# Projected q/k blocks: one ScalarE read of the PSUM bank, the rest formed by VectorE from the bank

## The reference, cut to what matters

```python
q = _split_heads(x @ Wq + bq)
k = _split_heads(x @ Wk + bk)
v = _split_heads(x @ Wv + bv)
scores = jnp.einsum('bhqd,bhkd->bhqk', q, k) / math.sqrt(HEAD_DIM)
```

## Time and profile before

| | value |
|---|---|
| median of 3 runs | 999.82 us |
| the profiled execution, its own time | 999.01 us |
| its span, first to last instruction | 997.1 us |
| TensorE matmul busy | 855.4 us (86%) |
| VectorE busy | 542.0 us (54%) |
| ScalarE busy | 421.5 us (42%) |
| GpSimd busy | 304.6 us (31%) |
| mean granted TensorE clock | 0.922 of full speed |

### The profile page before, as it was taken

The page is one execution under the profiler, slowest core; times in us unless marked ns, Lnnn a source line. Parts: engine busy times, 40 slices in busy tenths (PEclk is TensorE's granted clock), DMA queues, the critical chain, the costliest instruction groups (busy, mean ns, idle before and its releaser), DMA issues. The chain is left out here.

```text
span 997.1 us, 14099 instructions
## 1 busy us (share of the span) xinstructions
PE 855.4 (86%) x4842; PEld 541.8 (54%) x4842; DVE 542.0 (54%) x2095; ACT 421.5 (42%) x741; POOL 304.6 (31%) x365
## 2 busy tenths in 40 slices
PE   6979999898898899899889798349999999999940
PEld 2655556545455455355445243236877877877830
DVE  1268535779798799799878777410211211210136
ACT  1315434587585586686455556113021021022005
POOL 6113223434334333222253423460203212302332
PEclk9998999999799799899799689669999999999975
DMA  9652211202202202201321301631145135233242
GB/s 345 207 188 65 59 29 48 81 1 66 65 2 65 65 1 65 66 23 44 86 84 43 106 7 61 223 116 43 16 127 143 22 122 143 27 120 71 27 110 84
DMA packets 57510, 81.48 MB, mean 82 GB/s; under 512 B 6624, under 2 KB 51041, under 8 KB 55008
## 3 DMA queue, kind: packets, MB, share of 16 engines
q1 hardware_dynamic: 49520, 70.48, 22.0%
q0 software_dynamic: 7296, 9.47, 5.7%
q10 hardware_dynamic: 624, 0.63, 0.2%
HBM read 35.37 MB, written 19.68 MB: 55 GB/s over the span
## 5 line engine op out<-in xcount | busy, mean ns | idle before, releaser
L1102 DVE CUSTOM_DVE_ANT_0 junk<-ps,maskb 128x256 bf16<-128x256 f32 (+4 forms) x512 | 205.8, 434 | 66.3 <-PE ps L821 64.9
L647 ACT ACTIVATE probs<-ps 128x512 f32<-128x512 f32 (+1 forms) x304 | 157.4, 552 | 95.6 <-PE ps L844 91.3
L1559 PE MATMUL ps<-dxT,qs 128*128 128x320 f32 x512 | 141.1, 436 | 1.3 <-DVE dxT L1633 1.3
L1571 PE MATMUL ps<-ks,hTe 128*128 128x256 f32 x640 | 139.3, 379 | 0.0
L1593 ACT ACTIVATE hTe<-ps,qs 128x640 f32<-128x640 f32 x64 | 50.8, 793 | 204.6 <-PE ps L1559 204.6
L1515 POOL DMA_INDIRECT mixed_rows<-ysb,ids x40 | 61.7, 1543 | 228.1 <-DVE ysb L1653 225.2
L1571 PEld LDWEIGHTS ps<-ks,hTe 128*128 128x128 f32 x640 | 121.1, 190 | 16.3
L1559 PEld LDWEIGHTS ps<-dxT,qs 128*128 128x128 f32 x512 | 97.9, 192 | 42.5 <-DVE dxT L1633 1.9
L844 PE MATMUL ps<-qs,ks 99*128 99x256 bf16 (+4 forms) x512 | 107.7, 296 | 15.3 <-DVE nmax L1102 9.0
L821 PE MATMUL ps<-ks,qs 96*128 96x256 bf16 (+4 forms) x512 | 108.8, 299 | 12.6 <-DVE nmax L1102 7.3
L860 PE MATMUL ps<-probs,vaug 128*32 128x256 f32 (+4 forms) x1024 | 92.6, 437 | 6.2 <-POOL probs L557 5.6
(11 more groups left out here) (188 smaller groups left out, 1193.0 us busy)
## 6 DMA issues: line engine op xcount, KB each, us to landing
qs<-parts SPq DMA_DIRECT2D x96, 128.0 KB, 2.4
ks<-parts SPq DMA_DIRECT2D x96, 128.0 KB, 2.4
qs<-w SPq DMA_DIRECT2D x8, 1024.0 KB, 9.5
ks<-w SPq DMA_DIRECT2D x8, 1024.0 KB, 4.9
dispatched_rows<-att SPq DMA_DIRECT2D x8, 650.0 KB, 10.4
ks<-dispatched_rows SPq DMA_DIRECT2D x4, 650.0 KB, 7.2
x_sb<-xT SPq DMA_DIRECT2D x8, 256.0 KB, 3.9
mixed_rows<-h SPq DMA_DIRECT2D x4, 512.0 KB, 3.3
```

The costliest lines, as they stand in the source:

```text
L647: act.activation(probs_of(u)[:, heads[0]:heads[-1] + 1, :], turned_bank((u, half, i))[:, 0:len(heads) * w].rearrange("p (j n) -> p j n", n=w),
L1102: ins = dve.tensor_tensor_reduce(out=junk[:, b - (b > V_BANK), a * (hi - lo):(a + 1) * (hi - lo)], in0=score_bank((u, half, i))[:, a * (hi ...
L1559: ins = mm(bank(2 * (n % 2) + c)[:, 0:HC], w1s[:, e % 2, k, m * P:(m + 1) * P], dxT[:, e % 2, k, c * HC:(c + 1) * HC], start=(k == 0), sto ...
L1571: ins = mm(bank(4 + n % 2)[:, 0:D], hTe[:, e % 2, m, t * P:(t + 1) * P], w2s[:, e % 2, m, :], start=(m == 0), stop=(m == MH - 1))
```

## The change

ScalarE reads the bank once, into part 0, with the bias and without a scale; it no longer writes `proj` and no longer waits for `part2_done`. VectorE forms the rest straight from the bank, (bank + bias) - part 0, as one `scalar_tensor_tensor` into `proj`; that instruction now gives the bank free, and it takes over the wait for `part2_done`. The factor 1/4 goes into the q weights, which VectorE multiplies once per layer. Part 0 gets a semaphore of its own, on which SyncE and VectorE wait. The planner is told that a q/k bank is read one half later.

```diff
-READ_LATER = {"tok": {"h": 1}, "ffn": {"u": HIDDEN}, "gate": {"l": 1}, "route": {"c": 1}, "bias": {"o": 0}}
+READ_LATER = {"qkv": {"q": 1}, "tok": {"h": 1}, "ffn": {"u": HIDDEN}, "gate": {"l": 1}, "route": {"c": 1}, "bias": {"o": 0}}
...
                         if part == 0:
-                            sp.wait_ge(*d_out(("qkv", s, f"qk{i}")))
+                            sp.wait_ge(part0_done, 2 * NB * s + i + 1)
...
-                            pool.wait_ge(rest_done, n + 1)
+                            pool.wait_ge(*d_out(("qkv", i, f"qk{c - 2}")))
                             pool.tensor_copy(parts[:, c - 2, 1, :], proj[:, c % 2, :]).then_inc(part1_done, 1)
...
-                                if 2 * NB * i + j >= 2:
-                                    act.wait_ge(part2_done, 2 * NB * i + j - 1)
                                 if i:
                                     q = NB * (i - 1) + j // 2
                                     act.wait_ge(stack_in[q % NR], STACKED * (q // NR + 1))
-                                kw = dict(bias=ab[l][:, j:j + 1], scale=1.0 if j % 2 else DH ** -0.5)
-                                act.activation(proj[:, j % 2, :], dense_bank(key), ACT.Identity, **kw)
                                 act.activation(parts[:, j, 0, :], dense_bank(key), ACT.Identity,
-                                               **kw).then_inc(d_out(key)[0], 1)
+                                               bias=ab[l][:, j:j + 1]).then_inc(part0_done, 1)
...
-                                    if i == 0:
-                                        pe.wait_ge(for_a0, 16 * 2)
-                                    if i == B:
-                                        pe.wait_ge(for_rest, 16 * 9)
+                                    if i % B == 0:
+                                        pe.wait_ge(weights_scaled, l + 1)
...
-                                dve.wait_ge(*d_out(("qkv", i, f"qk{j}")))
-                                dve.tensor_tensor(proj[:, j % 2, :], proj[:, j % 2, :], parts[:, j, 0, :],
-                                                  ALU.subtract).then_inc(rest_done, 1)
+                                key = ("qkv", i, f"qk{j}")
+                                dve.wait_ge(part0_done, 2 * NB * i + j + 1)
+                                if 2 * NB * i + j >= 2:
+                                    dve.wait_ge(part2_done, 2 * NB * i + j - 1)
+                                dve.scalar_tensor_tensor(proj[:, j % 2, :], dense_bank(key), ab[i // B][:, j:j + 1],
+                                                         parts[:, j, 0, :], ALU.add, ALU.subtract
+                                                         ).then_inc(d_out(key)[0], 1)
...
+                                    dve.tensor_scalar(aw[1][:, :, 0:D], aw[1][:, :, 0:D], DH ** -0.5, None,
+                                                      ALU.mult).then_inc(weights_scaled, 1)
...
+                            dve.tensor_scalar(aw[0][:, :, 0:D], aw[0][:, :, 0:D], DH ** -0.5, None,
+                                              ALU.mult).then_inc(weights_scaled, 1)
```

More of the change, by code:

```diff
@@ L299, in build @@
         stack_in = [sem(f"stack_in{i}") for i in range(NR)]
-        rest_done, part1_done, part2_done, bias_added = (
-            sem(n) for n in ("rest_done", "part1_done", "part2_done", "bias_added"))
+        part0_done, part1_done, part2_done, bias_added, weights_scaled = (
+            sem(n) for n in ("part0_done", "part1_done", "part2_done", "bias_added", "weights_scaled"))
         ln_chain, var_done, rstd_done, ln_done = (sem(n) for n in ("ln_chain", "var_done", "rstd_done", "ln_done"))
```

## The result

The changed kernel takes **1029.79 us** (median of 4 runs, 1028.73 to 1032.16) against 999.4 (996.51 to 1000.0) for the kernel before: ratio 1.0312, 95% interval 1.0288 to 1.0335. The forecast was 1010.7, its range 994.5 to 1022. The direction was right; the loss is 30.4 us where 10.9 was forecast, and the time lies above the range.

The account below looks back on a forecast made before the run. TensorE and VectorE together were taken to bound projections 3 to 6. Terms -2.8 - 1.3 + 0.3 + 10.5 + 3.0 + 1.2 = +10.9 us on 999.01, plus 0.8 to the median, gave 1010.7 us, range 994.5 to 1022.

Parts of the forecast that it names:

- The mechanism: From projection 2 on, banks stay held until VectorE's rest, two halves on; planner told one, so TensorE and VectorE wait.
- same-half wait: Projections 3, 5, 6: five banks handed on in the half VectorE reads them; 2.1 us each, 10.5 us (0 to 15.5).
- next-half wait: Projections 4 to 6: six waits, bank handed on the half after VectorE's read; 0.5 us each, 3.0 us (0 to 14.4).
- VectorE's rest costs about the same: VectorE's 32 rests, now straight from the bank: 740 ns against 782, -1.3 us (-3.3 to +5.6).
- Weights: One VectorE instruction per layer scaling the q weights, hidden in layer 0: +0.3 us (0 to 0.69).
- ScalarE busy "some 22 us less": Profile sign: without 32 ScalarE reads of 684 ns, ScalarE's busy time falls by some 22 us.
- Projection 7: Turned scores wait for VectorE's rest while waits for GpSimd and ScalarE's second read go: +1.2 us (0 to 4.1).
- rival C: Much slower: new waits drop TensorE's clock to 1.2 GHz in a quarter of four stretches; 1023 us, chance 0.13.
- ScalarE's relief: ScalarE loses a read and a wait, returning VectorE's waits for it in projections 3 to 6: -2.8 us.
- small terms: Terms besides bank waits: ScalarE's lost read and wait -2.8, VectorE's rest -1.3, weight scaling +0.3 us.
- A: Faster: ScalarE was the hidden holder; half of TensorE's idle time in projections 3 to 7 returns, 995 us, chance 0.22.
- B: No change: bank waits come at half size and returned ScalarE time pays for them; 1000 us, chance 0.10.

Follow-up runs that it names:

- experiment 11: Kernel before, with only VectorE's rest put one half earlier in projections 2 to 7; ScalarE still reads twice: 996.61 us, ratio 0.9976.
- experiment 1: Changed kernel, planner told that q/k banks of projections 2 to 7 are read two halves later: 999.09 us, ratio 1.0002.
- experiment 2: Kernel before with only the new entry in the planner's table; ScalarE still frees the banks: 998.44 us, ratio 0.9995.
- experiment 3: Kernel before with the new table and the bank freed by VectorE's rest, old arithmetic and both ScalarE reads kept: 1032.09 us, ratio 1.0333.
- experiment 5: Changed kernel, planner never takes a bank in the half in which VectorE reads it, or sooner: 1012.08 us, ratio 1.0142.
- experiment 8: Changed kernel, planner told two halves for projections 2 to 7 except projection 6, told one: 1007.88 us, ratio 1.011.
- experiment 4: Kernel before without ScalarE's read into proj and its wait for part 2; rest formed from a constant tile: 995.03 us, ratio 0.9955.
- experiment 7: Changed kernel, rest formed one half after the product in projections 2 to 7, planner told two halves: 993.07 us, ratio 0.9938.
- experiment 6: Changed kernel, rest formed one half after the product instead of two in projections 2 to 7, table unchanged: 990.52 us, ratio 0.9933.
- experiment 9: Changed kernel, planner told two halves for projections 2 to 7 except projection 3, told one: 1004.33 us, ratio 1.0054.

## Why the prediction was right in direction and short in size

The mechanism came out as forecast; what failed is the size of its two terms, the price of a same-half wait and that of a next-half wait.

- **Mechanism and places: right.** The five same-half waits came where the table was worked through (951, 960, 866), projections 0 to 2 had none, and the next-half ones stand in projections 3 to 7. (The first three projections together are some 1.6 us longer in the profile after, but without a wait for the rest: the clock is at 0.51 from 82.4 to 85.9 us, and the profile of experiment 11, which is the kernel before in all but the place of the rest, has the same.) Experiments 1, 2 and 3 show that the hand-over table, with the late release, is the cause, and that neither alone is.
- **"VectorE's rest costs about the same": right,** 744 ns against 740, and none stretched to the 1.12 us of the earlier trace rows (735 to 751). Against the old rest where nothing stretched it (685 ns in the median) the new one is some 60 ns longer. Whether the bank or the bias pointer takes them no run separates. The rule on bank sources that the prediction cites from the Trainium skill ("VectorE: DVE Perf Modes", on the TRN2 errata) would give some 65 ns for the bank alone, an estimate from that page. The `tensor_tensor` speaks against it: 680 ns with a bank operand in the earlier trace rows, 681 after, and 685 with none.
- **Weights: at most +0.3, right:** 0.42 us at 23.8 and again at 55.4, and the halves of projection 0 start no later than before (its first maxima at 51.5 us, 51.9 before).
- **ScalarE busy "some 22 us less": not so.** It fell by 14.8 us, from 421.5 to 406.7, though all 32 reads of 684 ns are gone. In a row, ScalarE's instructions overlap: in the earlier trace rows the first read starts at 287.11 and takes 0.69, and the second starts at 287.70. The sum did not use this number.
- **Projection 7: right.** +1.2 forecast; it takes 0.9 us longer (35.09 against 34.14). TensorE's wait for the rest is 3.12 us there, VectorE's for GpSimd 3.07 (4.24 in the earlier trace rows).
- **Same-half waits: the term that failed first,** 10.5 forecast and 17.7 measured (by experiment 5, with five more next-half cases in exchange). The step was "the product takes 1.91 us and the first scores some 0.3". It holds where the clock stays (2.30 us in experiment 8, 1.8 us for each case of projection 3) and not where the clock falls during the wait, as in projections 5 and 6: there the product takes 3.5 to 3.8 us, VectorE idles 3.6 to 3.8, and a case costs 4.3 to 4.7. I had the clock, as rival C, but as a separate case with a chance of 0.13, while the waits of the forecast itself bring it about. C itself assumed 28 us at 1.2 GHz; by the granted clocks of the table after it was about 20, an estimate (twice 0.05 x 33.2 + 0.09 x 37.5 + 0.12 x 41.9). The upper end of the term, 15.5, was TensorE's lateness alone, with no slower product behind it.
- **Next-half waits: the term that failed most in proportion,** 3.0 (+1.2 in projection 7) forecast, 13.0 by experiments 5 and 1, which compare 22 such cases with 10, where the kernel after has 17. The step was the price of 0.5, argued from the shortness of the released product. The count was not too low: seven cases of over 1.5 us were forecast, and four came, beside seven shorter ones. Projection 4 shows the price by itself: three cases over 1.5 us were forecast there, at 1.5 us together; one came (2.36 us, with two of 0.19 and 1.23), and the stretch is 4.9 us longer. What counts is what TensorE has queued behind the wait, in order, that VectorE needs: 2.00 us behind the wait of 2.36, with the FFN product in between at the lower clock. How the rest of the 4.9 us arises was not followed up. The end of 14.4 was in the text; I chose the low end on the argument that an earlier wait had shifted TensorE already. That VectorE is shifted with it, as both are bound, would answer this; no run tests it.
- **ScalarE's relief: the size right (3.7 against 2.8), its sign in the sum not.** Experiment 4 has it with a bank free at once. In experiment 1, where the bank is held for two halves and nobody waits for it long, the whole change gives 0.3 us instead of the -3.8 that the small terms add up to. That holding the banks longer costs what the relief returns is the likely reading, but it is not shown: TensorE's waits for the rest there are only 2.4 us, and experiment 7, where banks are held longer than needed, can't be told from experiment 6.

17.7 + 13.0 + 0.3 = 31.0 is the way from the kernel after over experiments 5 and 1 back to the kernel before. It comes to the measured loss (30.4) by construction and is no test of the split.

The rivals: A (faster, TensorE's waits for the rest smaller than those for ScalarE) is out at 25.5 us of waits, where those for ScalarE's part 0 were 3.9 before, but its core, that ScalarE's early release and relief have a gain, shows as soon as the bank is free in time (experiments 4 and 6). B (no change) is what the kernel does once the table is right (experiment 1), not through returned time while it is wrong. C's mechanism, the fall of the clock, came together with the forecast's, and neither alone gives the measured time.

## What to carry to other kernels

When the reader of a buffer changes, find the step of the new reader **in the unit in which the planner counts**; here "one later" was one step and two halves. In a chain of two bound engines, price a wait not by its length nor by the operation it releases, but by all that is queued behind it in order, and at the lower clock where the waits themselves bring it down. If a resource is held too long, ask first whether its last reader can come sooner: one half sooner turned +30 us into -7 to -8, two halves sooner into +4 to +5.

## What the hardware showed that I had not expected

- With waits of 2.4 to 3.3 us the clock was at 1.2 GHz behind them and the product at nearly double length (3.49, 3.78, 3.78 us), and with others of 1.9 to 2.4 us it was not (projection 3, experiments 8 and 9). The wait's length alone doesn't tell which: 2.39 us is in both groups, 458.26 after and 436.87 in experiment 8.
- Useless work in the same gap saved more than it cost: transposes repeated to 3.74 us, in a time in which TensorE had to wait anyway, went with a product behind that was 1.8 us shorter.
- A `scalar_tensor_tensor` of 512 columns with a bank and a pointer scalar took 744 ns, a fifth below twice the 256-column one (479 ns each). GpSimd's masks do not stretch it: none of 32 took over 751 ns, and the one at 299.61 us took 0.74 beside a mask that ran from 299.11 to 300.19.
